# Two heads in one group of 32 rows, and six PSUM banks for the first projections of a 16-head attention stage

## The chip, the cores and the metric

The kernel runs on one core of a Trainium2 chip. The metric is device time in microseconds (us) of one execution: 4252.39 us is the median of three runs of the kernel before (4247.05 to 4257.46). One further execution was recorded by the hardware profiler; every row shown here is from that one. TensorE, the matrix engine, appears as PE (matmul) and PEld (weight load); VectorE is DVE, ScalarE is ACT, GpSimd is POOL, SyncE is SP, and SPq is the queue of SP's DMAs.

## The reference, cut to what matters

A decoder of two layers works on x of shape (4, 512, 256) in fp32: four batches of 512 tokens. Layer 0 has self-attention, cross-attention and a mixture of experts; layer 1 has the two attentions with 16 heads that the change is about, and then an MLP block of depth 6. Each step is followed by a layer norm over the sum with its input. The two attentions are the same computation, apart from mask, source and biases:

```
q = x @ Wq.T (+ bq)      k, v = src @ Wk.T (+ bk), src @ Wv.T (+ bv)      # src = x, or the context
split into 16 heads of 16 columns each
s = q_h @ k_h.T * 16 ** -0.5      # causal mask (self), or a mask from memory (cross)
a = softmax(s) ;  out = concat_h(a @ v_h) @ Wo.T (+ bo) ;  x = layernorm(x + out)
```

## The kernel before, in words

The stages run one after the other, each in a block of its own that all engines leave before the next begins: `stage_wide` (layer 0's attentions), `stage_moe`, `stage_heads` (layer 1's attentions, the stage of the change, L1716 on), `stage_l1_ffn`. Tokens stay in SBUF in `x_all`, 16 tiles of 128.

**stage_heads.** There are eight bodies: four batches of self-attention, then four of cross-attention. A body has 16 groups n = 0 to 15: four query tiles of 128 tokens, and per tile four groups of four heads. P is 128, QC (4) the groups of a tile, HPC (4) the heads of a group. A head has only 16 columns, but takes 32 rows of the array: the host spreads Wq, Wk and Wo so that 16 columns of a head are followed by 16 zeros (`spaced`, in `lay_out`). So q and k have 512 columns, in four projections of 128 ("q" and "k", L1930), each two fp32 matmuls of 128x512. v is not spread: a head's weights for the product with the probabilities are 32 columns of v (L1986), whose second half belongs to the next head; those rows of the output meet zeros in Wo. v's last 16 columns are a pad that DVE clears once (L2068), and PE begins the stage only when that is done (`pads`).

The order of the work is written by hand in `body()`: one list of steps, which each engine follows, doing the steps that are its own. In group n the steps are:

- **s**: PE, four score matmuls (L1954), one for each head, into banks 4 to 7. Each waits until DVE has emptied its bank.
- **max** 0 to 3: DVE adds the mask, copies to `prob` and takes the row maximum (L2121); after the fourth, `nb` (L2126) lets ACT begin the exponentials.
- **e** 0 to 3: ACT, the exponentials (L2049) of the group before (n - 1).
- **pt** 0 to 3: PE transposes the probabilities of group n - 2 (L1964) into banks 2 and 3 in turn; ACT copies pt 0 and 2 to SBUF, DVE pt 1 and 3 (L2017). pt 2 and 3 need the banks of pt 0 and 1.
- **pv**: PE multiplies the probabilities of group n - 3 with v (L1986) into bank 1.
- **first** (between pt 1 and pt 2, and on DVE between max 1 and max 2): a projection of q or k for the next body; or, where n % 4 is 3, **den** (PE spreads the reciprocal sums of a finished tile over rows, 4 matmuls, L1997) and **div** (ACT copies bank 1 to `o_raw`, L2064; DVE multiplies it with den's result into `oT`, L2148); or, where n % 4 is 0, **wo** (PE, four matmuls of 128x256 with Wo, L2008; DVE adds the result to `x_all`, L2155).
- **second** (after pt 3): half of the v projection (L1942), in groups 4 and 12.

For q there is a unit in groups 1, 5, 9 and 13, for k in 2, 6, 10 and 14. q, k, v, den and wo all use bank 0. The projections of the very first batch have no body beside them: they run in a phase of their own, with nothing but the steps of the next batch in it, one after the other in bank 0. PE fills, then ACT (q) or DVE (k, v) empties, then PE fills again. After the last body comes a short phase with the end of the last tile.

**Loads.** All weights are loaded by SP in one list (`load_later`, L2284) while `stage_wide` runs, in the order of the stages; `a1` and `x1` are those of `stage_heads`. After them SP loads the sources of `stage_wide`'s cross-attention (L1053), each when a mask buffer comes free.

```python
            for n in range(N):
                e, m = n - 1, n - 2
                ...
                yield ("s", 0, n)
                ...
                yield from [("max", 0, n, 0), ("max", 0, n, 1), ("pt", of(m), m, 0), ("e", of(e), e, 0),
                            ("e", of(e), e, 1), ("pt", of(m), m, 1), *first, ("max", 0, n, 2), ("max", 0, n, 3),
                            ("pt", of(m), m, 2), ("e", of(e), e, 2), ("e", of(e), e, 3), ("pt", of(m), m, 3), *second]
                ...
                yield ("pv", of(n - 3), n - 3)
```

Of the kernel before, what the change touches and what calls it, by code (L numbers as in the profile page):

```python
# [5 lines left out]
P = 128  # L6
# [1709 lines left out]
def stage_heads(nc, shared, w_self, w_cross, preload):  # L1716
# [3 lines left out]
    TB = 4  # L1720
# [5 lines left out]
    QC = H // HPC  # L1726
    N = TB * QC
# [3 lines left out]
    with ExitStack() as ctx:  # L1731
# [8 lines left out]
        qT = sb("qT", [P, 2, QC, S])  # L1740
        kT = sb("kT", [P, 2, QC, S])
        v = sb("v", [P, 2, TB, D + DH])
# [6 lines left out]
        rs_wide = sb("rs_wide", [P, H * ROWS])  # L1749
        o_raw = sb("o_raw", [P, QC * P])  # L1750
        oT = sb("oT", [P, QC * P])
# [21 lines left out]
        def body():  # L1773
# [54 lines left out]

        def cross(j):
            return j >= NB  # L1830
# [18 lines left out]
        def tile(j, t):  # L1849
            return j % NB * TB + t  # L1850

# [9 lines left out]
        def wait_drained_in_last_body(eng, ps, key, it):  # L1861
            n = ps.in_last_body(key, it)
            if n is not None:
                eng.wait_ge(shared["drained"][banks[key]], n)
# [34 lines left out]
        def _(pe):  # L1899
# [5 lines left out]
            for steps, ps, it in phases:  # L1905
                if it == NB - 1:
                    pe.wait_ge(w_cross["landed"], w_cross["loads"])
                for step in steps:
# [36 lines left out]
                    elif kind == "s":  # L1945
                        t, g = divmod(step[2], QC)
                        if t == 0:
                            wait_drained_in_last_body(pe, ps, ("q", 1, g), it)
                            wait_drained_in_last_body(pe, ps, ("k", 1, g), it)
                        for i in range(HPC):  # L1950
                            empty(step + (i,), it)
                        for i in range(HPC):
                            rows = slice(i * ROWS, (i + 1) * ROWS)
                            nc.tensor.matmul(ps.ap(step + (i,))[:, 0:keys(j, t)],  # L1954
                                             qT[rows, j % 2, g, t * P:(t + 1) * P], kT[rows, j % 2, g, 0:keys(j, t)],
                                             start=True, stop=True, tile_position=(i * ROWS, 0)
                                             ).then_inc(ps.sem_filled(step + (i,)), 1)
# [9 lines left out]
                    elif kind == "pv":  # L1967
# [15 lines left out]
                        for k in range(blocks):  # L1983
                            for i in range(HPC):
                                h = HPC * g + i
                                mm = nc.tensor.matmul(out[i * ROWS:(i + 1) * ROWS, g * P:(g + 1) * P],  # L1986
                                                      v[:, j % 2, k, h * DH:h * DH + ROWS],
                                                      pT[:, n % 2 * HPC + i, k * P:(k + 1) * P],
                                                      start=k == 0, stop=k == blocks - 1, tile_position=(0, i * ROWS))
                        if g == QC - 1:  # L1990
                            mm.then_inc(shared["filled"][1], 1)
                    elif kind == "den":
# [3 lines left out]
                        for g in range(QC):  # L1996
# [3 lines left out]
                    elif kind == "wo":  # L2000
# [6 lines left out]
                        for g in range(QC):  # L2007
                            mm = nc.tensor.matmul(ps.ap(step)[:, 0:D], oT[:, g * P:(g + 1) * P], w["Wo"][:, g, :],  # L2008
                                                  start=g == 0, stop=g == QC - 1)
# [10 lines left out]
        def _(act):  # L2020
            act.wait_ge(w_self["landed"], w_self["loads"])
            for steps, ps, it in phases:
                if it == NB - 1:
                    act.wait_ge(w_cross["landed"], w_cross["loads"])
                for step in steps:
# [27 lines left out]
                    elif kind == "den":  # L2053
# [10 lines left out]
                        nc.scalar.copy(o_raw[:], ps.tensor[:, 1, :]).then_inc(shared["drained"][1], 1)  # L2064

        @block.vector
        def _(dve):
            nc.vector.memset(v[:, :, :, D:D + DH], 0.0).then_inc(pads, 1)  # L2068
            dve.wait_ge(w_self["landed"], w_self["loads"])
            for steps, ps, it in phases:  # L2070
                if it == NB - 1:
                    dve.wait_ge(w_cross["landed"], w_cross["loads"])
                for step in steps:
# [11 lines left out]
                    elif kind == "v":  # L2085
                        i = step[2]
                        wait_filled(dve, ps, step, it)
                        out = v[:, j % 2, 2 * i:2 * i + 2, 0:D]
                        src = ps.ap(step).rearrange("p (t d) -> p t d", t=2)
                        if cross(j):  # L2090
                            ins = nc.vector.tensor_tensor(out, src, w_cross["bv"][:].unsqueeze(1).broadcast_to(
                                [P, 2, D]), ALU.add)
                        else:
                            ins = nc.vector.tensor_copy(out, src)
# [36 lines left out]
                    elif kind == "rs":  # L2131
# [3 lines left out]
                        nc.vector.reciprocal(rs[:], sums[:, t % 2, :]).then_inc(inverted, 1)  # L2135
                        dve.wait_ge(inverted, n)
                        nc.vector.tensor_copy(rs_wide[:].rearrange("p (h r) -> p h r", r=ROWS),
                                              rs[:].unsqueeze(2).broadcast_to([P, H, ROWS])).then_inc(rs_ready, 1)
                    elif kind == "div":
# [8 lines left out]
                        nc.vector.tensor_tensor(oT[:], o_raw[:], ps.ap(den), ALU.mult).then_inc(ps.sem_drained(den), 1)  # L2148
# [28 lines left out]
        def _(pool):  # L2177
            pool.wait_ge(w_cross["landed"], w_cross["loads"])
# [15 lines left out]
def mk_decoder(nc, ins, out):  # L2194
# [6 lines left out]
    with ExitStack() as ctx:  # L2201
# [16 lines left out]
        with ExitStack() as attention:  # L2218
# [13 lines left out]
            KC = D // P  # L2232
            for st, d, pre in (("a1", a1, "L1_attn_"), ("x1", x1, "L1_xattn_")):
                for n in ("Wq", "Wk"):
                    d[n] = weight(st, n, [P, KC, 2 * D], chunks(ins[pre + n]))
                d["Wv"] = weight(st, "Wv", [P, KC, D], chunks(ins[pre + "Wv"]))
                d["Wo"] = weight(st, "Wo", [P, 2 * KC, D], chunks(ins[pre + "Wo"]))
            x0["causal"] = weight("x0", "causal", [P, S // P, S], ins["causal"])
            a1["causal"] = x0["causal"]
            for n in ("bq", "bk"):  # L2240
                x1[n] = weight("x1", n, [P, 4], ins["L1_xattn_" + n])
# [38 lines left out]
            def load_later(sp, load_source):  # L2280
                for st in ORDER:
                    for of, dst, src in loads:
                        if of == st:
                            sp.dma_start(dst, src).then_inc(landed[st], 16)  # L2284
# [134 lines left out]
```

## Time and profile before

| | us |
|---|---|
| median of three runs | 4252.39 |
| profiled execution, its own time | 4249.61 |
| its span, first to last instruction | 4247.7 |
| PE busy in the span | 3943.0 |
| DVE busy | 2921.3 |
| ACT busy | 2606.4 |
| POOL busy | 1239.5 |
| PEld busy | 2603.9 |

The span is the time from the first to the last instruction of the execution; an engine's busy time is the sum of its own instructions. The stage of the change lies between 535 and 1290 us: the first phase from 535 to 566, the self-attention bodies to about 883, the cross-attention bodies to about 1280. A busy share says how full an engine is, not whether it sets the pace: that is read from the order of the instructions and from what each waited for. In the view by stretches the last three numbers of a row are the clock that TensorE was granted (1.00 is its full 2.4 GHz, 0.50 the half of it), the busy share of the DMA engines, and GB/s. In a timeline row, [0.86 <-DVE h_mx] says that the engine had been idle 0.86 us until DVE's h_mx released it. A matmul's row joins several records, two for an fp32 matmul; the next row of PE may begin before it ends, so what it costs is read from start to start.

### The profile page before, as it was taken

The numbers are of one execution on the slowest core, as the hardware profiler recorded it, in microseconds if no ns is written. First come the engines' busy times: TensorE is split into PE (matmuls) and PEld (weight loads), VectorE is DVE, ScalarE is ACT, GpSimd is POOL, SyncE is SP. The second block draws the span as 40 slices with busy tenths as digits, with TensorE's granted clock in tenths as the row PEclk, the third lists the DMA queues.
The fourth block names the chain that finished last, engine by engine and source line by source line (L and its number), as shares of the span: only waits on it lengthen the run. The fifth ranks groups of instructions, "written<-read, shape, count | busy, mean of one in ns | idle before, by whom it ended". The sixth has DMA issues, their size and how long they took to land.

```text
span 4247.7 us, 86120 instructions
## 1 busy us (share of the span) xinstructions
PE 3943.0 (93%) x30808; PEld 2603.9 (61%) x30808; DVE 2921.3 (69%) x10261; ACT 2606.4 (61%) x6872; POOL 1239.5 (29%) x809
## 2 busy tenths in 40 slices
PE   8979489899987999999999999999999999999986
PEld 5659346566664666666666666666666666666664
DVE  3542356777776877777777777777777777777773
ACT  2213146666674766777667667676667667676662
POOL 1103300000004433334343334343343434343330
PEclk9979799999998999999999999999999999999998
DMA  5002210000002000111011100111010100111010
GB/s 187 23 23 74 61 58 2 6 16 17 16 2 63 21 21 24 44 39 28 16 52 28 39 21 20 49 39 28 16 52 26 41 21 19 49 40 28 16 36 18
DMA packets 94306, 146.62 MB, mean 35 GB/s; under 512 B 17908, under 2 KB 59744, under 8 KB 93504
## 3 DMA queue, kind: packets, MB, share of 16 engines
q1 hardware_dynamic: 90480, 131.80, 10.7%
q0 software_dynamic: 3408, 9.31, 0.9%
q8 instruction: 254, 4.16, 0.4%
q14 instruction: 164, 1.34, 0.1%
HBM read 79.36 MB, written 11.40 MB: 21 GB/s over the span
## 4 chain that ended last, share of the span: by engine, by line
PE 54%; DVE 8%; POOL 4%; issue 2%; DMA 1%; ACT 0%; SPq 0%; DVEq 0%; POOLq 0%
PE psum L496 18%; PE psum L591 9%; PE psum L476 7%; PE psum L575 6%; PE psum L608 5%; PE psum L554 4%; PE psum L529 4%; POOL f_rn L898 3%; DVE f_rot L716 2%; DVE f_rot L718 1%; DVE f_ss L723 1%; DVE f_xn L813 1%; DVE f_prob L759 1%; PE psum L597 1%; DVE f_prob L787 1%
## 5 line engine op out<-in xcount | busy, mean ns | idle before, releaser
L496 PE MATMUL psum<-f_wqkv,f_xsT 128*128 128x512 f32 x2304 | 1077.9, 596 | 4.3 <-ACT f_raw L641 2.7
L893 POOL TENSOR_TENSOR f_raw<-f_rot 128x512 f32<-128x512 f32 x384 | 488.3, 1272 | 1690.4 <-DVE f_rot L718 1690.4
L655 ACT ACTIVATE f_prob<-f_prob,f_nb,f_rq 128x128 f32<-128x128 f32 x1536 | 744.7, 492 | 37.9 <-DVE f_nb L772 37.0
L496 PEld LDWEIGHTS psum<-f_wqkv,f_xsT 128*128 128x128 f32 x2304 | 401.0, 191 | 323.9 <-issue 319.3
L898 POOL TENSOR_TENSOR f_rn<-f_ss,f_half_pow 128x32 f32<-128x32 f32 x96 | 522.9, 5446 | 11.1
L759 DVE CUSTOM_DVE_ANT_0 f_prob<-psum,f_band 128x128 f32<-128x128 f32 x1536 | 353.6, 286 | 130.0 <-PE psum L529 128.8
L591 PE MATMUL psum<-f_xnT,f_w 128*128 128x512 f32 x960 | 437.5, 595 | 2.2 <-ACT f_hT L678 1.1
L639 ACT ACTIVATE f_sq<-psum 128x512 f32<-128x512 f32 x384 | 228.3, 594 | 227.8 <-PE psum L496 227.5
L787 DVE TENSOR_SCALAR f_prob<-f_prob,f_rs 128x128 f32<-128x128 f32 x1536 | 342.6, 287 | 13.6
L575 PE MATMUL psum<-f_wo,f_oT 128*128 128x256 f32 x1536 | 347.4, 379 | 1.7 <-ACT f_v L641 0.9
L716 DVE TENSOR_TENSOR f_rot<-f_raw,f_tab 128x512 f32<-128x512 f32 x384 | 333.7, 869 | 15.4 <-DMA x_before_mlp<-x_all 15.4
L575 PEld LDWEIGHTS psum<-f_wo,f_oT 128*128 128x128 f32 x1536 | 289.8, 190 | 71.3 <-issue 35.7
L2049 ACT ACTIVATE h_prob<-h_prob,h_nb 128x512 f32<-128x512 f32 (+3 forms) x512 | 325.8, 642 | 0.0
L591 PEld LDWEIGHTS psum<-f_xnT,f_w 128*128 128x128 f32 x960 | 179.0, 191 | 209.7 <-issue 200.5
L655 ACT ACTIVATION_READ_ACCUMULATOR f_prob<-f_prob,f_nb,f_rq 128x1 f32 x1536 | 299.4, 195 | 0.0
L666 ACT COPY f_oT<-psum 128x512 f32<-128x512 f32 x192 | 111.9, 583 | 282.3 <-PE psum L554 282.2
L1964 PEld LDWEIGHTS psum<-ident,h_prob 128*128 128x128 f32 x1664 | 184.8, 141 | 130.3 <-issue 66.0
L688 DVE COPY f_pT<-psum 128x512 f32<-128x512 f32 x192 | 132.0, 687 | 192.4 <-PE psum L476 192.2
L718 DVE TENSOR_TENSOR f_rot<-f_raw,f_tab 128x512 f32<-128x512 f32 x384 | 263.3, 686 | 0.0
L2017 ACT COPY h_pT<-psum 128x512 f32<-128x512 f32 (+3 forms) x256 | 129.6, 506 | 213.9 <-PE psum L1964 213.9
L723 DVE TENSOR_REDUCE f_ss<-f_sq 128x8 f32<-128x512 f32 x384 | 260.8, 679 | 0.0
L476 PE MATMUL psum<-ident,f_prob 128*128 128x128 f32 x1536 | 243.7, 281 | 9.6 <-DVE f_prob L787 9.3
(249 smaller groups left out, 7268.7 us busy)
## 6 DMA issues: line engine op xcount, KB each, us to landing
f_v_near<-f_v SPq DMA_DIRECT2D x168, 256.0 KB, 3.4
f_wqkv<-in_Wqkv SPq DMA_DIRECT2D x36, 512.0 KB, 5.9
w_moe_W<-in_L_ffn_W SPq DMA_DIRECT2D x2, 4096.0 KB, 21.9
f_w<-in_W SPq DMA_DIRECT2D x12, 640.0 KB
f_wo<-in_Wo SPq DMA_DIRECT2D x6, 1024.0 KB, 6.5
f_xs<-x_all SPq DMA_DIRECT2D x24, 254.0 KB
expert_rows<-m_y SPq DMA_DIRECT2D x39, 128.0 KB, 1.7
h_mask_int<-in_mask_BxSxS_ik SPq DMA_DIRECT2D x16, 256.0 KB, 2.6
```

Of the source, the lines that this page charges most:

```text
L476: mm = nc.tensor.transpose(ps.ap(key)[:, slot * P:(slot + 1) * P], src, ident[:])
L496: mm = nc.tensor.matmul(ps.ap(step), xsT[:, c, t * P:(t + 1) * P], wqkv[:, c, i * HALF:(i + 1) * HALF], start=c == 0, stop=c == KC - 1)
L575: mm = nc.tensor.matmul(ps.ap(step)[:, 0:D], oT[:, c, :], wo[:, c, :], start=c == 0, stop=c == OC - 1)
L591: mm = nc.tensor.matmul(ps.ap(step), w1[:, c, at:at + P], xnT[:, c, :], start=c == 0, stop=c == KC - 1)
L655: ex = nc.scalar.activation(pr, pr, ACT.Exp, bias=nb[:, t % 2, h:h + 1], scale=rq8[:, t, h:h + 1], accum_out=sums[:, t % 2, h:h + 1])
L716: nc.vector.tensor_tensor(heads(rot[:, n % 2, 0, :]), heads(q), cos, ALU.mult)
L718: nc.vector.tensor_tensor(rot[:, n % 2, 1, :].rearrange("p (h two d) -> p h two d", two=2, d=DH // 2), swapped, sin.rearrange("p h (two d) ...
L759: red = nc.vector.tensor_tensor_reduce(prob[:, (4 * n + 2 * j + i) % 16, :], ps.ap(key)[:, (n % 2 * 2 + j) * P:(n % 2 * 2 + j + 1) * P], b ...
L787: ins = nc.vector.tensor_scalar(pr, pr, rs[:, t % 2, h:h + 1], None, ALU.mult)
L893: nc.gpsimd.tensor_tensor(raw[:, (4 * t + i) % 8, :], rot[:, n % 2, 0, :], rot[:, n % 2, 1, :], ALU.add).then_inc(rope_done, 1)
L898: nc.gpsimd.tensor_tensor(rn[:, t % 2, :], ss[:, t % 2, :], half_pow[:], ALU.pow).then_inc(rn_ready, 1)
L2049: nc.scalar.activation(pr, pr, ACT.Exp, bias=nb[:, t % 2, h:h + 1], scale=scale, accum_out=sums[:, t % 2, h:h + 1]).then_inc(exp_ready, 1)
```

## The change: what it does

Two heads now share 32 rows. For q, the 16 columns of an even head and those of its odd neighbour lie side by side, so q has 256 columns (two projections of 128, PC = 2). k keeps its 512 columns: in a group for even heads the odd head's 16 rows are zeros, and in a group for odd heads the even head's are. v is kept twice, once with the columns of odd heads zero and once with those of even heads zero; two groups of heads add into the same 256 columns of bank 1. So `o_raw`, `oT`, `rs_wide` and Wo's rows shrink from 512 to 256 and from four chunks to two. POOL clears the whole of v (128 x 4096 fp32) at the stage's start in place of DVE's clear of the pad (128 x 128); PE and DVE wait for it. DVE writes each v result in two copies, one for each parity.

The q units of groups 5 and 13 are gone, the one of group 9 is q 1. The first phase's projections use banks 0, 4, 5, 6, 7, 1 in turn.

The host's layout stays. SP's loads pick the columns: Wq in 2 DMAs with pieces of 64 bytes, Wk in 8 with pieces of 128 bytes, Wo in 16 of 16 rows each (for each of the two attentions), and the biases bq and bk in 32 small DMAs.

```diff
-        v = sb("v", [P, 2, TB, D + DH])
+        v = sb("v", [P, 2, 2, TB, D])
...
-            units = {1: ("q", 0), 2: ("k", 0), 5: ("q", 1), 6: ("k", 1), 9: ("q", 2), 10: ("k", 2), 13: ("q", 3),
-                     14: ("k", 3)}
+            units = {1: ("q", 0), 2: ("k", 0), 6: ("k", 1), 9: ("q", 1), 10: ("k", 2), 14: ("k", 3)}
...
+        first_banks = {}
+        for step in full:
+            if step[0] in ("q", "k", "v") and step[1] == 1:
+                first_banks[step] = (0, 4, 5, 6, 7, 1)[len(first_banks) % 6]
...
-                    ps.fill(key, bank)
+                    ps.fill(key, first_banks.get(key, bank) if it < 0 else bank)
...
-                                mm = nc.tensor.matmul(out[i * ROWS:(i + 1) * ROWS, g * P:(g + 1) * P],
-                                                      v[:, j % 2, k, h * DH:h * DH + ROWS],
+                                pair = (g // 2 * HPC + i) * ROWS
+                                mm = nc.tensor.matmul(out[pair_rows(i), g // 2 * P:(g // 2 + 1) * P],
+                                                      v[:, j % 2, g % 2, k, pair:pair + ROWS],
                                                       pT[:, n % 2 * HPC + i, k * P:(k + 1) * P],
-                                                      start=k == 0, stop=k == blocks - 1, tile_position=(0, i * ROWS))
+                                                      start=g % 2 == 0 and k == 0,
+                                                      stop=g % 2 == 1 and k == blocks - 1,
+                                                      tile_position=(0, i * ROWS), skip_group_check=True)
...
                     elif kind == "den":
-                        for g in range(QC):
+                        for g in range(PC):
...
                     elif kind == "wo":
-                        for g in range(QC):
+                        for g in range(PC):
...
-                        nc.scalar.copy(o_raw[:], ps.tensor[:, 1, :]).then_inc(shared["drained"][1], 1)
+                        nc.scalar.copy(o_raw[:], ps.tensor[:, 1, 0:PC * P]).then_inc(shared["drained"][1], 1)
...
-            nc.vector.memset(v[:, :, :, D:D + DH], 0.0).then_inc(pads, 1)
+            dve.wait_ge(pads, 1)
...
-                        out = v[:, j % 2, 2 * i:2 * i + 2, 0:D]
+                        for parity in range(2):
+                            out = of_parity(v[:, j % 2, parity, 2 * i:2 * i + 2, :], parity)
...
-                                              rs[:].unsqueeze(2).broadcast_to([P, H, ROWS])).then_inc(rs_ready, 1)
+                                              rs[:].unsqueeze(2).broadcast_to([P, H, DH])).then_inc(rs_ready, 1)
...
-                        nc.vector.tensor_tensor(oT[:], o_raw[:], ps.ap(den), ALU.mult).then_inc(ps.sem_drained(den), 1)
+                        nc.vector.tensor_tensor(oT[:], o_raw[:], ps.ap(den)[:, 0:PC * P], ALU.mult).then_inc(ps.sem_drained(den), 1)
...
         def _(pool):
+            nc.gpsimd.memset(v[:], 0.0).then_inc(pads, 1)
...
+                d["Wq"] = sb(place, f"w_{st}_Wq", [P, KC, D])
+                for c in range(KC):
+                    rows_c = slice(c * P, (c + 1) * P)
+                    loads.append((st, d["Wq"][:, c, :].rearrange("p (h r) -> p h r", r=DH),
+                                  ins[pre + "Wq"][rows_c].rearrange("p (h two r) -> p h two r", two=2, r=DH)[:, :, 0]))
+                    for g in range(4):
+                        e, s = divmod(g, 2)
+                        loads.append((st, d["Wk"][:, c, g * P:(g + 1) * P].rearrange("p (i w) -> p i w", w=2 * DH),
+                                      ins[pre + "Wk"][rows_c, e * D:(e + 1) * D].rearrange("p (i w) -> p i w", w=4 * DH)
+                                      [:, :, s * DH:(s + 2) * DH]))
+                for h in range(H):
+                    e, j = divmod(h, HALF_HEADS)
+                    loads.append((st, d["Wo"][j * DH:(j + 1) * DH, e, :],
+                                  ins[pre + "Wo"][2 * h * DH:(2 * h + 1) * DH, :]))
```

## Rows read from the trace of the kernel before

**Rows 1.** Busy us (x count) by stretch: PE, PEld, DVE, ACT, POOL; then PEclk, DMA

```profile
724.00:803.00 79.00, 71.32 (x716) 47.64 (x712) 56.54 (x206) 51.62 (x168) 1.01 (x1) 1.00 0.01 2
980.00:1078.00 98.00, 91.58 (x999) 63.06 (x992) 77.14 (x213) 66.79 (x166) 3.47 (x2) 1.00 0.06 18
```

**Rows 2.** Timeline, cross-attention, groups 3 and 4: start, us, engine, what, [idle before]

```profile
1004.32 0.57 ACT L2064 COPY h_o_raw<-psum 128x512 f32<-128x512 f32 x1
...
1004.98 0.69 DVE L2148 TENSOR_TENSOR h_oT<-h_o_raw,psum 128x512 f32<-128x512 f32 x1 [1.18 <-ACT h_o_raw L2064]
...
1007.04 1.14 PE L1954 MATMUL psum<-h_kT,h_qT 32*128 32x512 f32 x8 [0.86 <-DVE h_mx L2121]
...
1009.04 1.89 PE L2008 MATMUL psum<-w_x_Wo,h_oT 128*128 128x256 f32 x8
...
1010.97 0.42 DVE L2155 TENSOR_TENSOR x_all<-psum,x_all 128x256 f32<-128x256 f32 x1 [0.75 <-PE psum L2008]
```

**Rows 3.** Groups of instructions by line and shape, whole span: busy, mean ns | idle before

```profile
L2148 DVE TENSOR_TENSOR h_oT<-h_o_raw,psum 128x512 f32<-128x512 f32 x32 | 22.0, 687 | 33.3 <-ACT h_o_raw L2064 30.2 <-PE psum L1997 2.5 <-issue 0.7
L2064 ACT COPY h_o_raw<-psum 128x512 f32<-128x512 f32 x32 | 18.3, 570 | 2.2 <-PE psum L1986 2.2
L2155 DVE TENSOR_TENSOR x_all<-psum,x_all 128x256 f32<-128x256 f32 x32 | 13.6, 425 | 28.0 <-PE psum L2008 28.0
L2017 ACT COPY h_pT<-psum 128x256 f32<-128x256 f32 x32 | 11.9, 373 | 22.5 <-PE psum L1964 22.5
L1997 PE MATMUL psum<-ident,h_rs_wide 128*128 128x128 f32 x256 | 33.9, 275 | 0.0
```

**Rows 4.** Timeline of PE alone, cross-attention, groups 9 and 10

```profile
1038.38 1.14 PE L1954 MATMUL psum<-h_kT,h_qT 32*128 32x512 f32 x8
...
1040.38 1.88 PE L1930 MATMUL psum<-h_xT,w_x_Wq 128*128 128x512 f32 x4
1042.10 1.04 PE L1964 MATMUL psum<-ident,h_prob 128*128 128x128 f32 x8
...
1044.08 1.14 PE L1954 MATMUL psum<-h_kT,h_qT 32*128 32x512 f32 x8
```

**Rows 5.** Timeline, last body, which projects nothing for a next one

```profile
1255.14 1.14 PE L1954 MATMUL psum<-h_kT,h_qT 32*128 32x512 f32 x8
...
1258.51 0.63 PE L1964 MATMUL psum<-ident,h_prob 128*128 128x128 f32 x4 [0.25 <-DVE h_pT L2017]
...
1260.08 1.14 PE L1954 MATMUL psum<-h_kT,h_qT 32*128 32x512 f32 x8
```

**Rows 6.** Timeline, the stage's start and the first batch's projections

```profile
535.06 0.17 DVE L2068 MEMSET h_v<- 128x128 f32 x1 [4.82 <-PEq L1328]
...
537.98 3.63 PE L1930 MATMUL psum<-h_xT,w_a_Wq 128*128 128x512 f32 x4 [0.72 <-issue]
...
542.28 1.98 PE L1930 MATMUL psum<-h_xT,w_a_Wk 128*128 128x512 f32 x4 [0.68 <-ACT h_qT L2039]
...
566.10 0.50 PE L1954 MATMUL psum<-h_kT,h_qT 32*128 32x128 f32 x8
```

**Rows 7.** Groups of instructions by line and shape, POOL

```profile
L2190 POOL TENSOR_TENSOR x_all<-x_all,w_x_bo 128x1024 f32<-128x1024 f32 x4 | 9.5, 2370 | 0.0
...
L1682 POOL IOTA m_cols_int<- 128x128 int32 x1 | 0.2, 240 | 1.7 <-POOLq L923 1.7
L1683 POOL IOTA m_token_int<- 128x16 int32 x1 | 0.1, 142 | 0.0
```

**Rows 8.** Timeline of SP's DMAs while the weights are loaded

```profile
29.88 13.95 SPq L2284 DMA_DIRECT2D w_a_Wq<-in_L_attn_Wq  x1
...
53.77 0.43 SPq L2284 DMA_DIRECT2D w_x_bo<-in_L_xattn_bo  x1
142.00 0.38 SPq L1053 DMA_DIRECT2D w_srcT<-in_ctxT  x1
```

**Rows 9.** DMA view, 536 to 540 us: queue: packets, MB, share of 16 engines

```profile
q1 hardware_dynamic: 765, 0.68, 53.2%
```

More of the change, by code:

```diff
@@ L1748, in stage_heads @@
         rs = sb("rs", [P, H])
-        rs_wide = sb("rs_wide", [P, H * ROWS])
-        o_raw = sb("o_raw", [P, QC * P])
-        oT = sb("oT", [P, QC * P])
+        rs_wide = sb("rs_wide", [P, PC * P])
+        o_raw = sb("o_raw", [P, PC * P])
+        oT = sb("oT", [P, PC * P])
         mask_int = sb("mask_int", [P, 2, S], mybir.dt.int32)
@@ L1850, in tile, with pair_rows @@
             return j % NB * TB + t
+        def pair_rows(i):
+            return slice(i * ROWS, (i + 1) * ROWS)
         def group(it, m):
@@ L1863, in wait_drained_in_last_body @@
             if n is not None:
-                eng.wait_ge(shared["drained"][banks[key]], n)
+                eng.wait_ge(shared["drained"][ps.previous.bank[key]], n)
         def out_key(m):
@@ L2087, in _ @@
                         wait_filled(dve, ps, step, it)
-                        out = v[:, j % 2, 2 * i:2 * i + 2, 0:D]
                         src = ps.ap(step).rearrange("p (t d) -> p t d", t=2)
[L2090 to L2094, printed above, removed]
+                        for parity in range(2):
+                            out = of_parity(v[:, j % 2, parity, 2 * i:2 * i + 2, :], parity)
+                            if cross(j):
+                                bias = w_cross["bv"][:].unsqueeze(1).broadcast_to([P, 2, D])
+                                ins = nc.vector.tensor_tensor(out, of_parity(src, parity), of_parity(bias, parity),
+                                                              ALU.add)
+                            else:
+                                ins = nc.vector.tensor_copy(out, of_parity(src, parity))
                         ins.then_inc(ps.sem_drained(step), 1)
@@ L2232, in mk_decoder @@
             KC = D // P
+            H, HALF_HEADS, DH = 16, 8, 16
             for st, d, pre in (("a1", a1, "L1_attn_"), ("x1", x1, "L1_xattn_")):
-                for n in ("Wq", "Wk"):
-                    d[n] = weight(st, n, [P, KC, 2 * D], chunks(ins[pre + n]))
+                d["Wq"] = sb(place, f"w_{st}_Wq", [P, KC, D])
+                d["Wk"] = sb(place, f"w_{st}_Wk", [P, KC, 2 * D])
+                d["Wo"] = sb(place, f"w_{st}_Wo", [P, KC, D])
+                for c in range(KC):
[11 more added lines that the diff above has]
+                                  ins[pre + "Wo"][2 * h * DH:(2 * h + 1) * DH, :]))
@@ L2236, in mk_decoder @@
                 d["Wv"] = weight(st, "Wv", [P, KC, D], chunks(ins[pre + "Wv"]))
-                d["Wo"] = weight(st, "Wo", [P, 2 * KC, D], chunks(ins[pre + "Wo"]))
             x0["causal"] = weight("x0", "causal", [P, S // P, S], ins["causal"])
             a1["causal"] = x0["causal"]
-            for n in ("bq", "bk"):
-                x1[n] = weight("x1", n, [P, 4], ins["L1_xattn_" + n])
+            x1["bq"] = sb(place, "w_x1_bq", [P, 2])
+            x1["bk"] = sb(place, "w_x1_bk", [P, 4])
@@ new lines, in mk_decoder @@
+            for h in range(H):
+                e, j = divmod(h, HALF_HEADS)
+                i, s = divmod(j, 2)
+                at, col = j % 4 * 2 * DH, 2 * e + j // 4
+                loads.append(("x1", x1["bq"][j * DH:(j + 1) * DH, e:e + 1],
+                              ins["L1_xattn_bq"][at:at + DH, col:col + 1]))
+                at = i % 2 * 4 * DH + s * DH
+                loads.append(("x1", x1["bk"][i * 2 * DH:(i + 1) * 2 * DH, 2 * e + s:2 * e + s + 1],
+                              ins["L1_xattn_bk"][at:at + 2 * DH, col:col + 1]))
@@ L2283, in load_later @@
                         if of == st:
-                            sp.dma_start(dst, src).then_inc(landed[st], 16)
+                            with nc.allow_non_contiguous_dma(reason="bias columns of 16 or 32 rows"):
+                                sp.dma_start(dst, src).then_inc(landed[st], 16)
                     if st == "a0":
```

20 lines of the change are left out of this document (12 added, 8 removed).

## The prediction, made before the changed kernel had run

> **What bounds the kernel now.** I read the busy times by stretches first. In a self-attention stretch of 79 us PE is busy 71.3 us, DVE 56.5 and ACT 51.6; in a cross-attention stretch of 98 us it is 91.6, 77.1 and 66.8, all at full clock [rows 1]. PE is the fullest engine, but it idles 6 to 8 us in each stretch, and with three engines that hand one group of heads round, an average does not say who is late. So I read the timelines, from one score step (s, L1954) to the next, because every group begins with one. The reader is to see four sorts of group.
>
> In a group with a q projection PE goes without a pause from s at 1038.38 to s at 1044.08, 5.70 us [rows 4]: PE sets the pace. The last body has no projections, and a plain group takes 1255.14 to 1260.08, 4.94 us [rows 5]. There the rows show a loop: pt 3 at 1258.51 waited for DVE to empty pt 1's bank, which DVE does only after two maxima; then pv, then s. That is the floor of a cross-attention group without extra work.
>
> In the group with den and div, DVE waits 1.18 us for ACT's copy of `o_raw` (1004.32), divides at 1004.98, takes its last two maxima, and PE's next s at 1007.04 had to wait 0.86 us for these [rows 2]. The path is ACT copy, DVE div, DVE max, PE s. Over the stage DVE's div waited 30.2 us for that copy and only 2.5 us for den on PE, in 32 tiles [rows 3]. In the group with wo, PE's wo runs from 1009.04, and DVE's add at 1010.97 had waited 0.75 us for it [rows 2]; over 32 tiles it waited 28.0 us, 0.875 us each [rows 3]. Here too PE ends last, inside the group.
>
> **The change part by part**
>
> *wo, two matmuls in place of four.* A row of four records with 512 columns each, q, costs 1.72 us from its start to the next row's (1040.38 to 1042.10) [rows 4]; wo has eight records of half the columns, the same stream, and 1.89 us against 1.88 of busy time [rows 2, 4]. Half of it is 0.86 us. DVE waited 0.875 us on average at this place [rows 3], so nearly all is taken off the path: I take 0.84. Where a v projection follows (two tiles of four), PE has no pause and gains it likewise. 31 of the 32 tiles end beside a body: 31 x 0.84 = 26.0 us. Bounds: 0, if in every group the loop through pt 3 is late at once, and 31 x 0.86 = 26.7. I take a value near the upper one, since the wait row is a sum over all tiles. What is late next is the loop through pt 3.
>
> *o_raw and div on 256 columns.* ACT's copy goes from 570 ns to the 373 ns of a 128x256 copy from PSUM, 0.20 less. DVE's div goes from 687 ns to the 425 ns of the add that reads a 128x256 result, 0.26 less [rows 3]; both are in the chain just read. Den's halving is worth little: DVE waited 2.5 us in all for it. I take 0.45 a tile: 31 x 0.45 = 14.0 us. Bounds: 0 and 31 x 0.46 = 14.3, the value near the upper one because the 1.18 us wait is larger than what the copy gives.
>
> *q, two units in place of four.* PE saves 2 x 1.72 us a body where it sets the pace, but the group then falls on the 4.94 us loop, so a cross-attention group gains 5.70 - 4.94 = 0.76 us [rows 4, 5]. In group 5 DVE also has the layer norm's statistics of the body before, which would be late next; I take 0.5 there. Three cross bodies project for a next one: 3 x 1.26 = 3.8 us. Four self-attention bodies do so too; their groups have shorter rows and PE is not fuller (71.3 of 79), and I take 0.4 for each unit as an estimate: 4 x 0.8 = 3.2 us. Sum 7.0 us; bounds 0 and 14 x 1.72 = 24.1 us. ACT loses 14 q copies beside that, hidden by its idle third [rows 1].
>
> *The first batch in six banks.* Before, q 0 starts at 537.98 and the first s at 566.10, with ten units in bank 0, each fill waiting for the emptying of the one before (k 0 at 542.28 waited for ACT's q copy) [rows 6]. Q 0's row lasts 3.63 us and k 0's 1.98: TensorE began at its lower clock. After: q 0 ends near 541.6, then seven units (five of q and k, two of v, which stream the same columns) follow without a pause, 7 x 1.72 = 12.0, to 553.6. The first s needs bank 4, which the last unit, k 3, now fills, so DVE's copy of it, 0.69, comes before: 554.4. That is 11.7 us sooner. Bounds: 13.4 us if the copy were hidden, 10.0 if k 0 too still ran at the lower clock, and 2 x 2.8 = 5.6 us (two of ten units less, at the old pace of 28.1 / 10) if the banks brought nothing.
>
> *The clear of v.* It moves from DVE (0.17 us) to POOL and grows to 4096 elements a partition, with PE and DVE queued behind it and nothing beside it. No row has a POOL clear of such a size. POOL's iota takes 142 ns for 16 elements and 240 for 128, that is 0.875 ns an element, or 3.6 us for 4096; its add with two inputs takes 2370 ns for 1024, 9.5 us for 4096 [rows 7]. The one that writes without reading is the nearer: 3.6, so 3.4 us are added, between 1.7 (if two elements went at a time) and 9.3.
>
> *v copies.* Two of 256 in place of one of 512 on DVE, about 0.1 us more each, 16 times, in groups in which PE's v unit and wo set the pace: nothing, 2 us if that cover is gone. `rs_wide` is shorter by some 0.14 us on DVE, beside PE's s: nothing. pv and s keep their number and shape.
>
> *The loads.* The weights of the two attentions go from 12 DMAs to 88: 27 for the first, 61 for the second with its 32 for biases. SP issues one in 0.43 us when nothing holds it, 0.47 from start to start, so 76 more are 36 us; its list ended at 54.2 us, and its next DMA was issued at 142.00 [rows 8]. It ends near 90: nothing. The engines have some 16,400 small pieces more; in a stretch with small packets 765 took 53.2% of 16 engines' 4 us, 44 ns each [rows 9], or 45 us with all sixteen, to about 99 us at worst. The stage itself starts at 535.
> The page "DMA: Bandwidth & Descriptors" (Specifications) of the Trainium skill asks for at least 512 bytes a piece for line rate and has the engines read, change and write below that; pieces of 64 and 128 bytes are what it warns of. Of this kernel's rows only those of rows 9 bear on it, and they leave the price hidden; by the rule the load would be slower, and the sum the same.
>
> *The end.* In the phase after the last body nothing lies beside: den 0.45 (half of its eight records [rows 3] of 128 columns and a load of 128 each, so half the columns of wo's), div 0.26, wo 0.86: 1.55 us.
>
> **The sum**, against the profiled execution: 26.0 + 14.0 + 7.0 + 11.7 - 3.4 + 1.55 = 56.9 us. Its own time was 4249.6, which gives 4192.7; the median of the runs was 4252.4, which gives 4195.5. I take 4194.
>
> **The rivals.** *PE sets the pace everywhere*: then each PE cut counts in full, 14 x 1.72 + 31 x (0.86 + 0.45) = 64.7, with start and end (8.3 + 1.55) 74.5 us: 4176. For it: PE is over 90% busy in cross-attention; against: the plain group of the last body, in which PE waits.
>
> *DVE's loop sets it*: wo's and q's cuts vanish, what stays is 14.0 + 8.3 + 1.55 = 23.9 us: 4227. For it: DVE's next maxima always wait on something that waited on DVE; against: the 28.0 us that DVE itself waited for wo.
>
> *The six banks don't overlap*, because the copies behind them are late or the clear on POOL is as slow as its add: the start then gives 5.6 - 9.3 = -3.7 in place of +8.3: 4206.
>
> *Slower, by the loads*: SP does the small DMAs one after the other, and the source of the second cross-attention batch of the first layer, at 142.00, stands behind them. One issue did take 13.95 us behind a full queue [rows 8]. It begins to cost when the 88 DMAs take over (142.0 - 29.9) / 88 = 1.27 us each; to eat the gain as well they would need (112 + 57) / 88 = 1.92 us, plus what slack the batch has. At 2.2 us each the stage before would start 82 us late: 4194 + 82 = 4276. Against: that one stood behind 4 MB loads of another stage, and the last of the list shows 0.43 again.
>
> **How the numbers follow.** The sum as worked out has 0.62, PE everywhere 0.10, DVE's loop 0.13, the start without gain 0.10, slower by the loads 0.05. The likeliest is 4194. The range goes from a little below PE everywhere to beyond the failed start, 4172 to 4218; left out are most of DVE's loop and the slower case. Chances: faster by over 0.2% (8.5 us, about what a measurement of this kernel can tell from none) 0.93, within it 0.02, slower 0.05.
>
> **What would show it.** From s to s, cross-attention: den groups near 5.9 (6.4 before), wo groups near 4.9, those of group 13 near 4.9 in place of 5.70. DVE's wait for wo near nothing; its wait for `o_raw` slightly smaller. The first s about 16 to 17 us after q 0's start, a POOL clear of 3 to 4 us before PE's first transpose, and the stage's loads done before 100 us. It is wrong if the cross groups keep their lengths with PE idle in them, if the clear takes over 6 us, or if a later s waits for a copy of the first phase.

## The result, and the profile after

The changed kernel takes 4191.72 us (median of four runs, 4189.01 to 4195.22), the kernel before 4250.8 us (four runs beside them, 4247.05 to 4257.46). The ratio is 0.9859, with a 95% interval of 0.9846 to 0.9872: 59 us faster, where 57 were forecast and 4194 us predicted. In the profiled executions the span fell from 4247.7 to 4190.6 us, by 57.1.

The stage's length is read from its first DMA (`f_rope`, L116) to DVE's first clear of the next stage (`f_kT`, L690): 534.97 to 1290.68 us before, 535.59 to 1233.37 after, so 755.7 and 697.8 us. So the stage gained 57.9 us, and the whole gain lies in it; "the stage" below is this length.

Busy time in one self-attention and one cross-attention stretch of the kernel after, each one body long; the columns are those of [rows 1]:

```profile
690.00:765.00 75.00, 66.57 (x691) 43.02 (x690) 55.66 (x214) 50.81 (x168) 1.01 (x1) 1.00 0.01 2
948.00:1042.00 94.00, 86.85 (x978) 58.52 (x977) 76.34 (x220) 66.29 (x169) 3.48 (x2) 1.00 0.06 18
```

Timeline of the kernel after, groups 3 (den) and 4 (wo) of the second cross-attention body, which answers to [rows 2]:

```profile
967.31 0.36 ACT L2074 COPY h_o_raw<-psum 128x256 f32<-128x256 f32 x1
...
967.75 0.42 DVE L2165 TENSOR_TENSOR h_oT<-h_o_raw,psum 128x256 f32<-128x256 f32 x1 [0.96 <-ACT h_o_raw L2074]
...
969.54 1.14 PE L1962 MATMUL psum<-h_kT,h_qT 32*128 32x512 f32 x8 [0.59 <-DVE h_mx L2136]
...
971.55 1.03 PE L2018 MATMUL psum<-w_x_Wo,h_oT 128*128 128x256 f32 x4
...
972.64 0.41 DVE L2172 TENSOR_TENSOR x_all<-psum,x_all 128x256 f32<-128x256 f32 x1
```

The groups of instructions over the whole span, which answer to [rows 3]:

```profile
L2165 DVE TENSOR_TENSOR h_oT<-h_o_raw,psum 128x256 f32<-128x256 f32 x32 | 13.5, 421 | 26.1 <-ACT h_o_raw L2074 21.5 <-issue 2.3 <-PE psum L2007 2.0
...
L2172 DVE TENSOR_TENSOR x_all<-psum,x_all 128x256 f32<-128x256 f32 x32 | 13.4, 419 | 2.6 <-PE psum L2018 2.6
...
L2074 ACT COPY h_o_raw<-psum 128x256 f32<-128x256 f32 x32 | 11.4, 355 | 2.0 <-PE psum L1994 2.0
...
L2007 PE MATMUL psum<-ident,h_rs_wide 128*128 128x128 f32 x128 | 19.6, 276 | 0.0
```

DVE's add no longer waits for wo: 2.6 us in all where it was 28.0. Its product still waits for ACT's copy, 21.5 us of 30.2: the copy and the product are shorter, the order is the same. PE is less full in both stretches and still at full clock.

The stage's start, which answers to [rows 6]:

```profile
535.60 3.51 POOL L2195 MEMSET h_v<- 128x4096 f32 x1 [6.14 <-POOLq L1328]
...
539.16 1.97 PE L1926 MATMUL psum<-ident,x_all 128*128 128x128 f32 x8 [68.61 <-POOL h_v L2195]
...
541.85 3.75 PE L1938 MATMUL psum<-h_xT,w_a_Wq 128*128 128x512 f32 x4 [0.72 <-issue]
...
545.40 2.21 PE L1938 MATMUL psum<-h_xT,w_a_Wk 128*128 128x512 f32 x4
...
557.96 0.69 DVE L2096 COPY h_kT<-psum 128x512 f32<-128x512 f32 x1 [0.96 <-PE psum L1938]
558.86 0.50 PE L1962 MATMUL psum<-h_kT,h_qT 32*128 32x128 f32 x8 [0.94 <-DVE h_kT L2096]
```

SP's loads, which answer to [rows 8], and the DMA view of 44 to 97 us with its small packets:

```profile
43.85 8.19 SPq L2326 DMA_DIRECT2D w_a_Wk<-in_L_attn_Wk  x4
...
96.30 0.43 SPq L2326 DMA_DIRECT2D w_x_bo<-in_L_xattn_bo  x1
140.49 0.38 SPq L1053 DMA_DIRECT2D w_srcT<-in_ctxT  x1
```

```profile
DMA packets 20901, 4.05 MB, mean 76 GB/s; under 512 B 18544, under 2 KB 20896, under 8 KB 20896
...
q1 hardware_dynamic: 20896, 3.99, 39.9%
```

The list ends at 96.7 us, 44 us before SP's next DMA.

From the starts of the score steps (s), the length of groups in the second cross-attention body, us; "wo" groups also hold a v unit where marked:

| group | before | after | wo_twice | div_wide | q_back | raw_early |
|---|---|---|---|---|---|---|
| 3 (den) | 6.39 | 5.90 | 5.91 | 6.38 | 5.91 | 4.87 |
| 4 (wo, v) | 7.43 | 6.63 | 7.43 | 6.62 | 6.62 | 6.65 |
| 5 (q before) | 5.70 | 4.90 | 4.90 | 4.89 | 5.70 | 4.90 |
| 6 (k) | 6.04 | 6.40 | 6.40 | 6.40 | 6.04 | 6.39 |
| 7 (den) | 6.39 | 5.90 | 5.90 | 6.38 | 5.90 | 5.48 |
| 8 (wo) | 5.78 | 4.92 | 5.79 | 4.92 | 4.92 | 4.93 |
| 13 (q before) | 5.70 | 4.90 | 4.89 | 4.90 | 5.70 | 4.89 |
| whole body | 100.29 | 93.93 | 97.12 | 95.85 | 95.17 | 90.45 |

### The profile page after: what moved, and what is told of

Read it like the earlier page. It is cut to its first block, busy times and chain, and to the rows that moved or that the text cites. A ratio compares the mean times of both kernels' runs of the same rounds, so it can differ in the third digit from the quotient of the medians.

```text
span 4190.6 us, 85556 instructions
## 1 busy us (share of the span) xinstructions
PE 3887.8 (93%) x30488; PEld 2558.7 (61%) x30488; DVE 2907.0 (69%) x10276; ACT 2577.9 (62%) x6856; POOL 1243.1 (30%) x810
## 4 chain that ended last, share of the span: by engine, by line
PE 55%; DVE 9%; POOL 4%; issue 2%; DMA 1%; ACT 0%; SPq 0%; DVEq 0%; POOLq 0%
PE psum L496 18%; PE psum L591 9%; PE psum L476 7%; PE psum L575 6%; PE psum L608 5%; PE psum L554 4%; PE psum L529 4%; POOL f_rn L898 3%; DVE f_rot L716 2%; DVE f_rot L718 1%; DVE f_ss L723 1%; DVE f_xn L813 1%; DVE f_prob L759 1%; PE psum L597 1%; DVE f_prob L787 1%
## 5 line engine op out<-in xcount | busy, mean ns | idle before, releaser
L1972 PE MATMUL psum<-ident,h_prob 128*128 128x128 f32 x1664 | 246.9, 279 | 30.0 <-DVE h_pT L2027 16.0
L476 PEld LDWEIGHTS psum<-ident,f_raw 128*128 128x128 f32 x1536 | 185.9, 141 | 108.2 <-issue 100.7
```

The costliest lines, as they stand in the source:

```text
L476: mm = nc.tensor.transpose(ps.ap(key)[:, slot * P:(slot + 1) * P], src, ident[:])
L1972: mm = nc.tensor.transpose(ps.ap(step)[:, k * P:(k + 1) * P], prob[:, n % 3 * HPC + i, k * P:(k + 1) * P], ident[:])
```

## The experiments

All edits start from the changed kernel. Each stood beside runs of the kernel before on the same chip. In the profiles the stage began anywhere between 531.1 and 542.3 us, though none of the edits touches what runs before it; so lengths of the stage, not of the span, are compared, and the medians are given with their ratio to before. The intervals of the ratios are 11 to 14 us wide, so by the times alone only wo_twice, div_wide, raw_early and all_moves are told from the changed kernel; the smaller differences rest on one profile each. What speaks for those profiles is that a group that no edit touches has the same length in all of them, mostly within 0.01 us, apart from the falls of the clock that the last section tells; the first phase differs by up to 0.3 us between profiles of the same code.

| kernel | median us | ratio to before (95%) | the stage, us | against the changed kernel's stage |
|---|---|---|---|---|
| changed | 4191.72 | 0.9859 (0.9846 to 0.9872) | 697.8 | |
| one_bank | 4197.68 | 0.9883 (0.9868 to 0.9899) | 703.8 | +6.1 |
| wo_twice | 4214.34 | 0.9929 (0.9916 to 0.9943) | 724.3 | +26.5 |
| den_twice | 4189.5 | 0.9865 (0.985 to 0.988) | 698.9 | +1.1 |
| div_wide | 4203.8 | 0.9902 (0.9886 to 0.9917) | 713.0 | +15.2 |
| q_back | 4197.61 | 0.9885 (0.9868 to 0.9901) | 706.6 | +8.9 |
| clear_hidden | 4185.4 | 0.9856 (0.984 to 0.9873) | 694.2 | -3.6 |
| ln_moved | 4191.36 | 0.9871 (0.9854 to 0.9887) | 700.1 | +2.3 |
| both_moved | 4187.55 | 0.9855 (0.9837 to 0.9873) | 694.1 | -3.7 |
| raw_early | 4164.89 | 0.9803 (0.979 to 0.9817) | 672.1 | -25.7 |
| start_and_ln | 4184.05 | 0.9847 (0.9834 to 0.9861) | 691.4 | -6.4 |
| all_moves | 4158.84 | 0.979 (0.9776 to 0.9803) | 664.9 | -32.9 |

**one_bank: are the six banks worth anything?**

```diff
-                    ps.fill(key, first_banks.get(key, bank) if it < 0 else bank)
+                    ps.fill(key, bank)
```

> The changed kernel with the first phase's eight projections all in bank 0 again; all else as changed. Theory (the six banks remove a fill-empty-fill chain, worth 2.8 us a unit against 1.72): from q 0's start to the first score step 8 x 2.8 = 22.4 us in place of the 17.0 that the changed kernel's trace shows, so about +5.5 us, 4197. Rival (the banks bring nothing, the shorter phase comes from two units less alone): no change, 4192, first score step 17 us after q 0.

Measured: +6.1 us of stage; the first score step came 29.3 us after the stage's first DMA (534.12 to 563.47), 23.3 in the changed kernel. PE alone, one_bank:

```profile
540.38 3.75 PE L1938 MATMUL psum<-h_xT,w_a_Wq 128*128 128x512 f32 x4 [0.72 <-issue]
544.80 1.98 PE L1938 MATMUL psum<-h_xT,w_a_Wk 128*128 128x512 f32 x4 [0.67 <-ACT h_qT L2049]
547.67 2.00 PE L1950 MATMUL psum<-w_a_Wv,h_xT 128*128 128x256 f32 x8 [0.88 <-DVE h_kT L2096]
...
563.47 0.50 PE L1962 MATMUL psum<-h_kT,h_qT 32*128 32x128 f32 x8
```

Each unit waits for the copy of the one before, as in the kernel before. The theory holds and the rival falls.

**wo_twice, den_twice, div_wide: which of the shrunk steps was on the path?**

```diff
# wo_twice
-                        for g in range(PC):
+                        for g in list(range(PC)) * 2:
                             mm = nc.tensor.matmul(ps.ap(step)[:, 0:D], oT[:, g * P:(g + 1) * P], w["Wo"][:, g, :],
# den_twice
-                        for g in range(PC):
+                        for g in list(range(PC)) * 2:
                             mm = nc.tensor.matmul(ps.ap(step)[:, g * P:(g + 1) * P], rs_wide[:, g * P:(g + 1) * P],
# div_wide: o_raw and oT are P x QC * P, den has QC matmuls (rs_wide's chunk g % PC), and
-                        nc.scalar.copy(o_raw[:], ps.tensor[:, 1, 0:PC * P])
+                        nc.scalar.copy(o_raw[:], ps.tensor[:, 1, :])
-                        nc.vector.tensor_tensor(oT[:], o_raw[:], ps.ap(den)[:, 0:PC * P], ALU.mult)
+                        nc.vector.tensor_tensor(oT[:], o_raw[:], ps.ap(den), ALU.mult)
```

> The changed kernel with wo's two matmul pairs done twice into the same place, so PE spends on wo what it did before the change (eight records a tile), and everything behind it keeps its size. Theory (wo on PE is on the path, shortened until the loop through pt 3 takes over): the groups with wo go back by 0.7 to 0.87 us each, 31 of them, and 0.86 at the end: +26 us, 4218; DVE's wait for wo before the add back near 28 us. Rival 1 (the DVE loop sets every group): under +3 us. Rival 2 (PE sets the pace everywhere): +27.5 us, which this run alone does not tell from the theory.

> The changed kernel with den's matmuls done twice, eight records a tile as before the change. Theory (the groups with den wait for ACT's copy and DVE's product, so den lies beside it): +0.45 us at the stage's end and nothing else, 4192, groups with den still 5.90 us in cross-attention. Rival (PE sets the pace everywhere): 32 x 0.45 = +14.4 us, 4206.

> The changed kernel with den (four matmuls), ACT's copy of o_raw and DVE's product at their old width of 512 columns; wo, q and the rest as changed. Theory (ACT copy, DVE product, DVE maxima, PE scores is the chain of that group): cross-attention groups with den 6.38 us again in place of 5.90, in all 31 x 0.48 + 0.9 at the end = +15.8 us, 4207. Rival (these widths are hidden, the groups shrank because PE had less to do): +0.5 us if den is hidden as well; with den_twice beside it the share of the two copies is told from den's.

Measured: +26.5, +1.1 and +15.2 us of stage. DVE's wait for wo in wo_twice, its wait at the product in den_twice, and product and copy in div_wide, over the whole span:

```profile
L2172 DVE TENSOR_TENSOR x_all<-psum,x_all 128x256 f32<-128x256 f32 x32 | 13.6, 425 | 28.0 <-PE psum L2018 28.0
```

```profile
L2165 DVE TENSOR_TENSOR h_oT<-h_o_raw,psum 128x256 f32<-128x256 f32 x32 | 13.5, 421 | 26.6 <-ACT h_o_raw L2074 23.9 <-PE psum L2007 2.5
```

```profile
L2166 DVE TENSOR_TENSOR h_oT<-h_o_raw,psum 128x512 f32<-128x512 f32 x32 | 22.0, 687 | 33.0 <-ACT h_o_raw L2075 29.8 <-PE psum L2007 2.5 <-issue 0.7
L2075 ACT COPY h_o_raw<-psum 128x512 f32<-128x512 f32 x32 | 18.2, 569 | 2.0 <-PE psum L1994 2.0
```

Wo_twice restores exactly the 28.0 us of [rows 3]. Only the wo groups grow, and group 4 of the first body, by 0.97 us, in which no wo stands: the trace has wo's matmuls in 30 groups beside the bodies (the first body has them in groups 8 and 12 alone) and those of two tiles in the phase at the end. Without it wo is worth 25.5 us. Den_twice leaves every cross-attention den group at 5.90; of its 1.1 us, 0.98 lie in the same group 4 (5.26 us for 4.28), which has no den either, 0.45 in the phase at the end, and the first phase was 0.3 shorter. The last section shows what group 4's 0.97 is. So all but the end's 0.45 of what div_wide adds is the two copies. This sinks "PE sets the pace everywhere" (den would have cost 14 us) and "DVE's loop sets it" (wo would have cost nothing).

**q_back: what was a q unit worth?**

```diff
-            units = {1: ("q", 0), 2: ("k", 0), 6: ("k", 1), 9: ("q", 1), 10: ("k", 2), 14: ("k", 3)}
+            units = {1: ("q", 0), 2: ("k", 0), 5: ("q", 2), 6: ("k", 1), 9: ("q", 1), 10: ("k", 2), 13: ("q", 3), 14: ("k", 3)}
# PE projects chunk e % PC again; ACT copies q 2 and q 3 to a spare tile; not present in the first phase
```

> The changed kernel with two more q units in groups 5 and 13 of each body that projects for a next one (not in the first phase): PE recomputes q 0 and q 1, ACT copies them to a spare tile. Theory (a q unit costs what PE's group takes beyond the 4.9 us loop, less what DVE's layer norm takes over in the group behind): from the groups of the two traces 3 x 1.24 in cross-attention and 4 x 1.1 in self-attention, +8 us, 4200. Rival 1 (PE sets the pace everywhere): 14 x 1.72 = +24 us, 4216. Rival 2 (the DVE loop sets it): 0.

Measured: +8.9 us, 0.98 of it in group 4 of the first body again. The cross bodies grow by 1.25 us, the self-attention ones by 0.98 to 1.20. In group 5 of the cross bodies the unit costs 0.80, and group 6 gives 0.36 back, as it took it in the change. Both rivals (24 and 0) are far off.

**clear_hidden, ln_moved, both_moved: two things that the change made worse**

```diff
# clear_hidden: PE's wait for pads at the stage's start is gone, DVE's stands before its first copy into v
+                        if j == 0 and i == 0:
+                            dve.wait_ge(pads, 1)
# ln_moved
-                if n == 5:
+                if n == 6:
-                    yield ("ln", -1)
-                if n == 6:
-                    yield from [("norm", -1), ("bo", 1)]
+                    yield from [("ln", -1), ("bo", 1)]
+                if n == 10:
+                    yield ("norm", -1)
```

> The changed kernel in which PE no longer waits for POOL's clear of v, and DVE waits for it only before its first copy into v, some 10 us later. Theory (the clear is 3.5 us on the path to the first transpose and nothing else): PE's first transpose right at the stage's start, -3.4 us, 4188. Rival (something else is ready only later, such as the clock or POOL's sharing of memory with DVE): under 1 us.

> The changed kernel with the layer norm's statistics behind group 6 in place of group 5, and its last step behind group 10 in place of 6. Theory (group 6 grew from 6.04 to 6.40 us in cross-attention because DVE comes to its maxima late from the statistics, 1.9 us, once q 1 no longer covers them): group 6 back at 6.04 or less, groups 7 and 11 at 5.90, since DVE waits there for ACT anyway; -0.36 x 3 in cross bodies, some 0.3 to 0.5 in each other body, -3 us in all, 4189. Rival (group 6 is longer for another reason, such as k's matmul): group 6 stays at 6.40, and groups 7 and 11 get longer: 0 to +5 us.

> Clear_hidden and ln_moved together. Theory: the two are far apart and add, -6.5 us against the changed kernel, 4185. Rival (one of them does nothing): -3 to -4 us.

Clear_hidden did what was expected, -3.6 us of stage. POOL and PE at its start:

```profile
531.07 3.51 POOL L2195 MEMSET h_v<- 128x4096 f32 x1 [6.14 <-POOLq L1328]
531.36 1.94 PE L1925 MATMUL psum<-ident,x_all 128*128 128x128 f32 x8 [65.30 <-PEq L1328]
```

Ln_moved is a miss. Group 6 fell to 6.03 us in cross-attention, as said, so DVE's statistics were what had lengthened it. But group 7 rose from 5.90 to 6.16, and in the second and third self-attention bodies from 4.08 to 4.54. DVE alone in ln_moved, group 7:

```profile
988.85 1.39 DVE L2176 BATCH_NORM_STATS2 h_stat<-x_all 128x6 f32<-128x256 f32 x4
990.28 0.38 DVE L2180 BATCH_NORM_AGGREGATE h_mv<-h_stat 128x2 f32<-128x6 f32 x4
990.69 0.17 DVE L2183 TENSOR_SCALAR h_rstd<-h_mv 128x4 f32<-128x4 f32 x1
990.81 0.69 DVE L2136 CUSTOM_DVE_ANT_0 h_prob<-psum,h_add_mask 128x512 f32<-128x512 f32 x1
...
992.64 0.41 DVE L2165 TENSOR_TENSOR h_oT<-h_o_raw,psum 128x256 f32<-128x256 f32 x1
```

The score step began at 988.28, and DVE came to its first maximum at 990.81, 2.5 us later, where 1.2 to 1.3 is usual. The 0.94 us for which DVE would have waited for ACT was used up, and the product came late without any wait in front of it. A wait of 0.96 us can hide 0.96 us, not 1.3. Of the +2.3 us in the table, 2.6 are two falls of TensorE's clock that the last section tells, so the edit itself was worth about nothing where -3 had been expected. Both_moved, without these falls, says the same: -3.7 us against the changed kernel and -0.1 against clear_hidden, so its rival holds (one of the two does nothing) and the two together don't give the 6.5 expected. Group 8 of the second body, 4.18 us in ln_moved and 3.94 in both_moved at full clock, shows that 0.2 us can differ without a cause that was found.

**raw_early, start_and_ln, all_moves: what the chain that was read allows**

```diff
# raw_early: ACT's copy of o_raw is a step of its own, right after s
                 yield ("s", 0, n)
+                if n % 4 == 3:
+                    yield ("raw", of((n - 7) // 4), (n - 7) // 4 % TB)
# start_and_ln: as clear_hidden, and
-                first_banks[step] = (0, 4, 5, 6, 7, 1)[len(first_banks) % 6]
+                first_banks[step] = (4, 5, 6, 7, 4, 5, 0, 1)[len(first_banks)]
# ... with ln behind group 9 and norm behind group 10; all_moves: both
```

> The changed kernel with one step of ACT moved: in the groups with den and div, ACT copies o_raw at the group's start, before its copy of pt 0 (for which it waits 1 us anyway), and not after two exponentials. Den, div and all sizes stay. Theory (these groups last 5.90 us because DVE's product waits 0.94 us for that copy): DVE waits no more, the group falls to the loop through pt 3, 4.9 us in cross-attention: 31 x about 0.9 = -28 us, 4163. Rival (PE sets the pace, or the product would then wait for den on PE): under -5 us.

> The changed kernel with three small moves: the clear of v off PE's path as in clear_hidden; the first phase's eight projections in banks 4, 5, 6, 7, 4, 5, 0, 1, so that the first score step need not wait for DVE's copy of the last k (it waited 0.94 us); the layer norm's statistics behind group 9, a group with q in which PE sets the pace, and its last step behind group 10. Theory: -3.4 - 0.9 at the start (19.0 us from the stage's first DMA to the first score step, 23.3 in the changed kernel), group 6 from 6.40 to 6.04 in cross-attention with groups 7 and 11 unchanged at 5.90 (unlike ln_moved, where group 7 grew to 6.16), -2 us in all bodies: 4185. Rival (a layer norm costs the same wherever it stands): group 10 or 11 grows by what group 6 gives, -4.3 us, 4187.5.

> Raw_early and start_and_ln together. Theory: with groups 7 and 11 no longer waiting for ACT, DVE's last step of the layer norm behind group 10 is no longer absorbed in group 11 and costs up to 0.7 us a body; else they add: -28 - 6 + 4 = -30 us, 4161, the fastest of all. Rival: no faster than raw_early alone.

Raw_early took 25.7 us off the stage, for 28 expected. Timeline, group 3 of the second cross-attention body, and the product's row:

```profile
955.59 0.36 ACT L2076 COPY h_o_raw<-psum 128x256 f32<-128x256 f32 x1
...
957.12 0.59 ACT L2029 COPY h_pT<-psum 128x512 f32<-128x512 f32 x1 [1.18 <-PE psum L1974]
...
958.43 0.41 DVE L2167 TENSOR_TENSOR h_oT<-h_o_raw,psum 128x256 f32<-128x256 f32 x1
...
960.23 1.14 PE L1964 MATMUL psum<-h_kT,h_qT 32*128 32x512 f32 x8
```

```profile
L2167 DVE TENSOR_TENSOR h_oT<-h_o_raw,psum 128x256 f32<-128x256 f32 x32 | 13.2, 413 | 2.4 <-PE psum L2009 2.0
```

The copy now lies where ACT waited for PE, and DVE's product waits for nothing in this group, and for PE alone in the sum, 2.0 us. Group 3 is 4.87 us, the loop through pt 3. Group 7, with DVE's last step of the layer norm in it, stops at 5.48, and in the second to fourth self-attention bodies it gives only 0.02 to 0.23 us, where most groups with den give 1.0: that is where the missing 2 us are.

Start_and_ln gave -6.4 us. The first score step came 18.7 us after the first DMA (532.25 to 550.91); group 6 fell to 6.04, and groups 7 and 11 stayed at 5.90. The statistics stand in a group where PE's q unit sets the pace: the rival (a layer norm costs the same wherever it stands) falls for bodies with a q unit, and holds in the last one, where group 10 rose to 5.80 as group 6 fell to 4.90. All_moves is the fastest, 4158.84 us, 2.1% below the kernel before; its stage lost 32.9 us, for 30 expected. Its group 11 is 5.48 us, the layer norm's 0.6 that was expected, but group 7, freed of that step, fell to 4.87, which the expectation had left out.

## Why the prediction was right

Each term against what was measured for it alone:

| term | predicted us | measured us | by |
|---|---|---|---|
| wo, with its part at the end | 26.0 + 0.86 | 25.5 | wo_twice, less the 0.97 of group 4 of the first body |
| copies and den, with their part at the end | 14.0 + 0.7 | 15.2 | div_wide |
| q | 7.0 | 7.9 | q_back, less the 0.98 of the same group |
| start: banks and fewer units, less the clear | 8.3 | 7.9 | 31.1 us to the first s before, 23.3 after |
| sum | 56.9 | 56.5, stage 57.9 | |

The mechanism is right term by term, but that the sums meet within 1 us is in part luck: the terms are off by 1.4, 0.5, 0.9 and 0.4 us, with different signs. The 1.4 us that the terms leave of the stage are known in part: 0.6 is the first phase, which the three edits don't touch and which was 0.13 to 0.27 us shorter in each of their profiles, and 0.35 lie in group 8 of the last body, which took 6.14 us before, 5.79 in wo_twice and 4.93 after. Why that group gained more than wo was not found.

*wo.* Named as the wait that ends last in its group, at 0.84 each; the wo groups lost 0.81 to 0.86 us in cross-attention, 0.72 in group 0, where the transposes for the next batch follow, and 1.21 in that one group 8; in self-attention they lost 0.66 to 0.86. The count was off by one: 30 wo groups lie beside bodies and two tiles' wo at the end, not 31 and one, which hardly changes the sum. The wait row of [rows 3] was the right evidence: a sum over all tiles of the wait that the shortened step ends.

*o_raw and div.* 0.45 each forecast, 0.48 to 0.49 measured, since ACT's copy took 355 ns and not the 373 of the neighbouring row. Den was said to be hidden but at the end; den_twice shows it. The lower bound given for these two terms was zero; for wo it was to hold "if in every group the loop through pt 3 is late at once", which it never was.

*q.* 0.76 a group forecast, 0.80 measured. That DVE's layer norm would take part of it back was said, but for group 5 and with 0.26; it took 0.36, and in group 6. In self-attention the estimate of 0.4 a unit was too low; 0.5 to 0.6.

*The start.* The banks were put at 11.7 with the two units less. One_bank separates them: 6.1 us from the banks, and 31.1 + 3.4 - 29.3 = 5.2 from fewer units (5.6 by the old pace). K 0 still ran partly at TensorE's lower clock, 2.21 us for 1.88; the bound for that had been 1.7 us, 0.3 came. The clear took 3.51 us for 3.6, the nearest row by kind (POOL's iota, per element) having been the right one, and the add with two inputs nowhere near. A row that bears on it was overlooked: DVE clears 128x1024 in the same trace in 912 ns (L690), which makes about 3.6 us for 4096, an estimate from another engine.

*The loads.* Hidden, as said, but later than said: 96.7 us for 90. The first Wk pieces took SP 8.19 us for four, and the whole stretch moved 76 GB/s; a packet took 0.399 x 16 x 53 us / 20,896 = 16 ns, where 44 had been taken as the upper price. The page "DMA: Bandwidth & Descriptors" (Specifications) of the Trainium skill wants pieces of at least 512 bytes for line rate. The trace agrees in direction: between 43 and 54 us the engines moved 393 GB/s before, at a busy share of 1.08, and 200 after, at 0.78. Nobody waited for it here.

*The clock.* It rested at full in the bodies of the profiled run, though PE became emptier.

The prediction did not say that DVE's wait of 1.18 us for ACT was itself avoidable; it used it only as cover. Raw_early shows that it was worth nearly half as much again as the whole change.

## What to carry to other kernels

Where several engines hand one small group of work round, measure from one fixed step to the same step of the next group, sort the groups by what is in them, and price a cut by the group's next-longest loop (4.9 us here), not by the engine's busy time. A wait that a profile sums over all its instances (28.0 us for wo, 30.2 for the copy) told here about what removing it gave: 25.5 us by the shorter wo, 25.7 by the earlier copy. And before shortening such a step, ask whether its engine could do it earlier, in an idle time that it has anyway. What is moved into a wait is free only up to the length of that wait.

## What the runs showed of the hardware that was not expected

TensorE's granted clock fell to half for 3 to 4 us inside the stage in four of the profiles, at the same place in the first body. The window of q_back at 568 to 569 us, and of the changed kernel, which comes to that place 2.4 us later, at 569 to 571, in the order of engines of [rows 1]:

```profile
568.00:569.00 1.00, 0.77 (x4) 0.55 (x4) 1.00 (x6) 1.00 (x7) 0.00 (x0) 0.50 0.00 0
```

```profile
569.00:571.00 2.00, 1.50 (x19) 0.66 (x11) 1.24 (x8) 1.71 (x10) 0.00 (x0) 1.00 0.03 8
```

Where it fell, in den_twice, q_back, ln_moved and wo_twice, group 4 of the first body (with a v unit, and neither wo nor den) took 5.25 to 5.27 us in place of 4.28. The changed kernel and the other seven variants show 1.00 from 565 to 570 us, and that group at 4.25 to 4.28. Ahead of it lie groups of 128 keys, in which PE has short transposes and waits. In ln_moved it also fell in the third body, at 735 to 737 us, where group 8 took 5.57 us for 3.94. So a difference of one or two microseconds between two profiles of such kernels may be the clock alone, and the groups' lengths tell it.

What each engine does in the first body up to that group is the same in these four, in the changed kernel, in div_wide and in raw_early, so the edits don't explain it. What the four share is when their stage began: 533.37 to 533.79 us after the span's start, and no other profile's began later than 532.25 and earlier than 534.12. Four profiles show that the two go together, not why; and whether the pauses that the change made have to do with the fall was not tried.
